# One buffer order for rotary and softmax, and the first key pair's rotation behind the second projection

## The reference, cut to what matters

```python
q = proj(Wq, bq); k = proj(Wk, bk); v = proj(Wv, bv)
q = _apply_rotary(q, cos, sin)      # per head, pairs of features
k = _apply_rotary(k, cos, sin)
attn = softmax(q @ k.T * scale)     # per head, 2048 x 2048
out = attn @ v
x = layernorm(x + out @ Wo.T + bo)
x = layernorm(x + moe(x))
```

## Time and profile before

| what | value |
|---|---|
| executions | 3115.75 and 3014.53 us, median 3065.14 |
| profiled execution | 3015.46 us; span of its slowest core (2) 3013.9 us |
| spans of the cores | 3002.6 to 3013.9 us, clock 0.950 to 0.953 |
| busy, core 2 | TensorE 2559.5 us (85%), VectorE 771.3 (26%), ScalarE 591.8 (20%), GpSimd 172.7 (6%) |
| chain that ended last | TensorE 74%, DMA 9%, VectorE 8%, issue 5%, ScalarE 4% |

### The profile page before, as it was taken

The page is one execution under the profiler, slowest core; times in us unless marked ns, Lnnn a source line. Parts: engine busy times, 40 slices in busy tenths (PEclk is TensorE's granted clock), DMA queues, the critical chain, the costliest instruction groups (busy, mean ns, idle before and its releaser), DMA issues.

```text
span 3013.9 us, 31163 instructions; the slowest of 8 cores (3002.6 to 3013.9 us)
## 1 busy us (share of the span) xinstructions
PE 2559.5 (85%) x12262; PEld 1189.2 (39%) x12262; DVE 771.3 (26%) x1140; ACT 591.8 (20%) x761; POOL 172.7 (6%) x323
## 2 busy tenths in 40 slices
PE   4778787888888888898499998999999899998993
PEld 3334343534353535343144443434444344443441
DVE  0222222222222222222722213131221312212226
ACT  0342424242424242432000000000000000000031
POOL 1000000000000000000001001010000101001000
PEclk9899999999999999998699999999999999999996
DMA  8310101010101010034034344444444444343423
GB/s 149 49 29 15 28 15 29 15 28 15 28 15 28 15 28 8 8 56 77 14 57 76 63 78 63 72 72 67 75 65 76 65 70 74 61 80 60 74 42 122
DMA packets 50720, 155.26 MB, mean 52 GB/s; under 512 B 6162, under 2 KB 6290, under 8 KB 49298
## 3 DMA queue, kind: packets, MB, share of 16 engines
q0 software_dynamic: 47264, 142.69, 29.0%
q1 hardware_dynamic: 3314, 10.59, 1.0%
HBM read 287.54 MB, written 8.39 MB: 98 GB/s over the span
## 4 chain that ended last, share of the span: by engine, by line
PE 74%; DMA 9%; DVE 8%; issue 5%; ACT 4%; DVEq 0%; ACTq 0%; POOL 0%; POOLq 0%
PE pb L792 15%; PE pb L809 14%; PE pb L866 9%; DMA wslab<-w_t 6%; PE pb L318 6%; PE pb L401 6%; PE pb L395 6%; PE pb L450 4%; PE pb L472 4%; PE pb L478 4%; PE pb L555 4%; DMA R_bf<-x_t 2%; ACT scr_bf L361 2%; ACT scr_bf L461 1%; DVE vbuf L639 1%
## 5 line engine op out<-in xcount | busy, mean ns | idle before, releaser
L866 PE MATMUL pb<-aog,wslab 128*128 128x512 bf16 x2048 | 458.5, 380 | 59.6 <-DMA wslab<-w_t 59.4
L792 PE MATMUL pb<-xy,wslab 128*128 128x512 bf16 x2048 | 466.2, 387 | 0.0
L809 PE MATMUL pb<-xy,wslab 128*128 128x512 bf16 x2048 | 452.5, 379 | 0.0
L803 ACT ACTIVATE scr_bf<-pb 128x512 bf16<-128x512 f32 x128 | 69.5, 594 | 1324.6 <-PE pb L792 1324.5
L866 PEld LDWEIGHTS pb<-aog,wslab 128*128 128x128 bf16 x2048 | 195.3, 98 | 319.2 <-issue 98.0
L461 ACT ACTIVATE scr_bf<-pb,mq_sb 128x1024 bf16<-128x1024 f32 x256 | 283.5, 1114 | 166.2 <-PE pb L478 114.4
L792 PEld LDWEIGHTS pb<-xy,wslab 128*128 128x128 bf16 x2048 | 203.0, 100 | 252.5 <-issue 20.7
L395 PE MATMUL pb<-R_bf,wslab 128*128 128x512 bf16 x768 | 293.4, 382 | 5.4 <-ACT vbuf L306 5.4
L809 PEld LDWEIGHTS pb<-xy,wslab 128*128 128x128 bf16 x2048 | 200.4, 98 | 241.6
L401 PE MATMUL pb<-R_bf,wslab 128*128 128x512 bf16 x768 | 293.1, 382 | 0.0
L879 DVE TENSOR_TENSOR R_f<-pb,R_f 128x512 f32<-128x512 f32 x256 | 177.1, 692 | 343.2 <-PE pb L866 329.9
(11 more groups left out here) (111 smaller groups left out, 1473.9 us busy)
## 6 DMA issues: line engine op xcount, KB each, us to landing
wslab<-w_t POOLq DMA_DIRECT2D x128, 512.0 KB, 5.6
wslab<-w_t POOLq DMA_DIRECT2D x128, 256.0 KB, 3.8
wslab<-wv_t POOLq DMA_DIRECT2D x8, 1024.0 KB, 9.3
R_bf<-x_t POOLq DMA_DIRECT2D x16, 512.0 KB, 7.2
wslab<-wq_t POOLq DMA_DIRECT2D x8, 1024.0 KB, 9.8
wslab<-wk_t POOLq DMA_DIRECT2D x8, 1024.0 KB, 9.7
wslab<-wo_t POOLq DMA_DIRECT2D x16, 512.0 KB, 5.3
y<-R_f SPq DMA_DIRECT2D x16, 512.0 KB, 2.6
```

Of the source, the lines that this page charges most:

```text
L792: last = t.matmul(pa[nc2].ap(), wslab.ap()[:, W1OFF[s1] + dc * 128: W1OFF[s1] + dc * 128 + 128], xy.ap()[:, dc * TL + nc2 * 512: dc * TL + ...
L809: last = t.matmul(pa[4 + nc2].ap(), wslab.ap()[:, W3OFF[s1] + dc * 128: W3OFF[s1] + dc * 128 + 128], xy.ap()[:, dc * TL + nc2 * 512: dc * ...
L866: last = t.matmul(pa[wb + nc2].ap(), wslab.ap()[:, W2OFF[s2] + fc * 128: W2OFF[s2] + fc * 128 + 128], aog.ap()[:, fc * TL + nc2 * 512: fc ...
```

## The change

- `emit_tail_pair` and `emit_evac_pair` use sb2 and sb3 for the evacuated pair and sb0 and sb1 for its squares, for all pairs.
- The tail of key pair 0 is issued behind the 32 matmuls of pair 2 and ahead of that pair's evacuation, no longer inside the matmuls.
- In `st_merged` the exponential of chunk kc writes the half kc % 2 (before: the other one), and is issued right behind scores(kc). TensorE's order becomes scores(0), scores(1), sums(0), then scores(kc), sums(kc-1), and at the end sums(15).

The number and the shapes of all instructions stay the same. The diff, cut to its core:

```diff
--- before.py
+++ after.py
@@ emit_tail_pair
-                    qso = 1024 if (a // 2) % 2 == 0 else 0
-                    qk = ["sb2", "sb3"] if qso else ["sb0", "sb1"]
...
-                            scr_bf.ap()[:, qso + q2 * 512: qso + q2 * 512 + 512],
+                            scr_bf.ap()[:, 1024 + q2 * 512: 1024 + q2 * 512 + 512],
...
-                            r=[qk[q2], "pswap"], w=[f"pa{2 + q2}"])
+                            r=[f"sb{2 + q2}", "pswap"], w=[f"pa{2 + q2}"])
...
-                        scr_f.ap()[:, 1024:2048], scr_bf.ap()[:, qso:qso + 1024],
+                        scr_f.ap()[:, 1024:2048], scr_bf.ap()[:, 1024:2048],
...
@@ emit_evac_pair
-                    A(lambda s, pbt=pbt, qso=qso: s.activation(
-                        scr_bf.ap()[:, qso:qso + 1024], pbt.ap(), AF.Identity,
+                    A(lambda s, pbt=pbt: s.activation(
+                        scr_bf.ap()[:, 1024:2048], pbt.ap(), AF.Identity,
...
-                        r=pbkeys + [bckey], w=qk)
+                        r=pbkeys + [bckey], w=["sb2", "sb3"])
+                    V(lambda v: v.tensor_tensor(
+                        scr_bf.ap()[:, 0:1024], scr_bf.ap()[:, 1024:2048],
+                        scr_bf.ap()[:, 1024:2048], ALU.mult),
+                        r=["sb2", "sb3"], w=["sb0", "sb1"])
...
@@ loop over pairs, behind T(pmm, ...)
-                        if dc == 2 and pr >= 1:
-                            emit_tail_pair(a - 2)
+                    if pr >= 1:
+                        emit_tail_pair(a - 2)
                     emit_evac_pair(a, pb_[pb[0] // 2],
                                    [f"pa{pb[0]}", f"pa{pb[1]}"])
@@ st_merged, emit_exp
-                    so = (1 - j) * 1024
...
-                        w=[f"sb{2 * (1 - j)}", f"sb{2 * (1 - j) + 1}"])
+                        w=[f"sb{2 * j}", f"sb{2 * j + 1}"])
...
@@ st_merged, order
                 emit_mms(0)
                 emit_mms(1)
                 if pre is not None:
                     pre()
                 emit_exp(0)
+                emit_exp(1)
+                sums_pvs(0)
                 for kc in range(2, NDC):
                     emit_mms(kc)
-                    emit_exp(kc - 1)
-                    if kc >= 2:
-                        sums_pvs(kc - 2)
-                emit_exp(NDC - 1)
-                sums_pvs(NDC - 2)
+                    emit_exp(kc)
+                    sums_pvs(kc - 1)
                 sums_pvs(NDC - 1)
```

More of the change, by code:

```diff
@@ L344, in emit_tail_pair @@
                         r=["pa2", "pa3", "sk"], w=["sf0", "sf1"])
-                    V(lambda v, a=a, qso=qso, cos=cos: v.tensor_tensor(
-                        scr_f.ap()[:, 1024:2048], scr_bf.ap()[:, qso:qso + 1024],
+                    V(lambda v, a=a, cos=cos: v.tensor_tensor(
+                        scr_f.ap()[:, 1024:2048], scr_bf.ap()[:, 1024:2048],
                         cos.ap()[:, a * 512: a * 512 + 1024], ALU.mult),
-                        r=qk + ["ck"], w=["sf2", "sf3"])
+                        r=["sb2", "sb3", "ck"], w=["sf2", "sf3"])
                     V(lambda v, a=a: v.tensor_tensor(
@@ L356, in emit_evac_pair @@
                 def emit_evac_pair(a, pbt, pbkeys):
[L357 to L360, removed]
-                    A(lambda s, pbt=pbt, qso=qso: s.activation(
-                        scr_bf.ap()[:, qso:qso + 1024], pbt.ap(), AF.Identity,
-                        bias=bcol.ap()[:, hh:hh + 1]),
-                        r=pbkeys + [bckey], w=qk)
[L365 to L368, removed]
+                    A(lambda s, pbt=pbt: s.activation(
+                        scr_bf.ap()[:, 1024:2048], pbt.ap(), AF.Identity,
+                        bias=bcol.ap()[:, hh:hh + 1]),
+                        r=pbkeys + [bckey], w=["sb2", "sb3"])
[3 more added lines that the diff above has]
+                        r=["sb2", "sb3"], w=["sb0", "sb1"])
                     for q2 in range(2):
-                        T(lambda t, q2=q2, sqo=sqo: t.matmul(
+                        T(lambda t, q2=q2: t.matmul(
                             pa[4 + q2].ap(), ones_sq.ap(),
-                            scr_bf.ap()[:, sqo + q2 * 512: sqo + q2 * 512 + 512],
+                            scr_bf.ap()[:, q2 * 512: q2 * 512 + 512],
                             start=True, stop=True),
-                            r=[sk_[q2], "ones"], w=[f"pa{4 + q2}"])
+                            r=[f"sb{q2}", "ones"], w=[f"pa{4 + q2}"])
                     if nt == 2:
@@ L445, in st_merged, with sums_pvs @@
             def st_merged(pre=None):
+                def sums_pvs(kc):
+                    j = kc % 2
+                    for qb in range(2):
+                        T(lambda t, kc=kc, j=j, qb=qb: t.matmul(
+                            pa[6 + qb].ap(), ones_sq.ap(),
+                            scr_bf.ap()[:, j * 1024 + qb * 512:
+                                        j * 1024 + qb * 512 + 512],
+                            start=(kc == 0), stop=(kc == NDC - 1),
+                            skip_group_check=True),
+                            r=[f"sb{2 * j + qb}", "ones"], w=[f"pa{6 + qb}"])
+                        T(lambda t, kc=kc, j=j, qb=qb, hl=hl: t.matmul(
+                            pa[4 + qb].ap(),
+                            vbuf.ap()[:, kc * 256 + hl * 128:
+                                      kc * 256 + hl * 128 + 128],
+                            scr_bf.ap()[:, j * 1024 + qb * 512:
+                                        j * 1024 + qb * 512 + 512],
+                            start=(kc == 0), stop=(kc == NDC - 1),
+                            skip_group_check=True),
+                            r=[f"sb{2 * j + qb}", f"vb{kc}"], w=[f"pa{4 + qb}"])
                 def emit_mms(kc):
@@ L459, in emit_exp @@
                     j = kc % 2
-                    so = (1 - j) * 1024
-                    A(lambda s, j=j, so=so: s.activation(
-                        scr_bf.ap()[:, so:so + 1024],
+                    A(lambda s, j=j: s.activation(
+                        scr_bf.ap()[:, j * 1024:(j + 1) * 1024],
                         pb[j].ap(), AF.Exp, bias=mq_sb.ap()[:, 6:7],
```

2 lines of the change are left out of this document (1 added, 1 removed).

## The result

| | before | changed kernel |
|---|---|---|
| median of the timed executions | 3015.6 us | 3065.4 us |
| profiled execution, span of the slowest core | 3013.9 us | 3065.6 us |
| median span of die 0, die 1 | 3011.5, 3005.0 | 3058.1, 3061.1 |

The ratio is 1.0171 with a 95% interval of 1.0158 to 1.0184, so the change costs about 51 us. I had forecast 3060 and a range of 3036 to 3082. Both executions timed before the prediction had left 3065 as the median of before; with more of them it is 3015.6, the profiled execution's time, so the sum had been made against the right number.

A forecast was written before the change was run, and what follows sets the result against it. TensorE, the fullest engine, was taken as the bound, losing time to waits behind the second key projection; 16 x (2.5 + 0.3 + 0) = 45 us on 3015.5 gave 3060 us, range 3036 to 3082.

The forecast's parts named there:

- part 1: Tail moved behind the second key projection: evacuation waits for cosine, square behind the add; each head 2.50 us later.
- ones-matmuls' wait: Sign: TensorE's wait for the square behind the second key projection grows by 16 x about 2.5, to 145 us.
- The 0.3 us for ones-matmuls at the low clock: Behind the second key projection: ones-matmuls run slow after longer TensorE idle time, +0.3 us a head.
- part 4: TensorE's clock: falls earlier behind the second key projection; ones-matmuls +0.3 us a head, low stretch in the loop 0.
- bounds of -1.4 and +1.0: Loop's low-clock stretch, us a head: ending at the same time gains 1.4, wholly covered by matmuls loses 1.0.
- +0.42 in place of +0.3: Ones-matmuls behind the second key projection wholly at the low clock, by the skill's rule; us a head, sum 3062.
- 2.5 to 3 us later after its last projection matmul: Sign: a head's first exponential comes this much later, otherwise the prediction is wrong as a whole.
- within 2%: Whole kernel's time differs from before by at most 2%, about 60 us; chance 0.79.
- clearly slower by the clock: Rival: ones-matmuls all at low clock, loop's low stretch fully covered; 63 us, 3079; chance 0.17.
- half of it back: Rival: the loop's low-clock stretch ends at the same time, so the loss is 22 us, 3038; chance 0.12.
- a tighter loop: Rival: exponentials issued in the order of their scores tighten the chunk loop; 45 - 37 = 8 us, 3024; chance 0.06.
- a hidden tail: Rival: evacuation and square behind the second key projection don't wait for the moved work; 3015; chance 0.03.

The follow-up runs named there:

- `loop_only`: Kernel before with only the new order of exponential and sums in the loop over chunks; spans of 3007.7 to 3010.9 us.
- the two filled kernels: Kernel before and changed kernel, each with useless matmuls in all of TensorE's gaps in a head; profiled executions 2986.0 and 3030.6 us.
- `tail_only`: Kernel before with only the tail of key pair 0 moved behind the 32 matmuls of pair 2; ratio 1.0184.
- `halves_only`: Kernel before with only the buffer edit: every pair evacuated into sb2 and sb3 and squared into sb0 and sb1; ratio 0.9997.
- `after_dc2`: Changed kernel with the tail of key pair 0 put back behind dc 2, the other two edits kept; ratio 1.0007.

## Why the prediction was right or wrong

**What was right.** The place of the loss (behind the second key projection), its sign, and its largest term: 37.4 of the 50.1 us are the delay of the square, where 2.5 a head gives 37.5. The steps of part 1 came out to a few hundredths in the head shown: sine 0.99 us behind the last projection matmul (0.98 forecast), cosine 1.14 behind it, evacuation 3.44 behind the last projection matmul (3.44 forecast), ones-matmuls' wait 146.0 us (145). The add had the longer gap of 0.46 us in this head, so its square is 2.77 late (3.20 behind the last projection matmul, which itself comes 0.43 earlier); most heads have the short gap (in two places only of the 48 adds was there an idle time). The 0.3 us for ones-matmuls at the low clock came out at 0.25 a head. One half for all pairs cost nothing alone. The loop cost nothing where it starts at the low clock (`loop_only`), and 0.13 us a head between the two filled kernels.

**A cause named in the wrong order.** I led with the evacuation that waits for the shared half, and noted the queue of VectorE beside it, with both ready 0.02 us apart. `tail_only` shows that the queue alone gives the delay, all but 0.06 us a head. The number was the same; the reason would have misled someone who then gave the evacuation a buffer of its own.

**What was wrong: the size of the clock's term, and what I took for measurable.** The sum had 0.3 us a head for ones-matmuls at the low clock and 0 for the rest of the clock, 4.5 us in 15 heads. It is 10.4. The step that failed is the "I take 0" of part 4: it looked only at the long gap and at where the one low stretch of a head would begin and end. The two things it asked about came out near the sum: the ones-matmuls cost 3.7 us (4.5 forecast), and the low stretch in the loop cost 5.1 us less than before, 0.34 a head and well inside the bounds of -1.4 and +1.0. What it had no term for is the projections, where low stretches that before doesn't have cost 11.8 us, behind short gaps as the 2.15 us after the query that had been harmless. Filling only those gaps took them away. That a later arrival moves every gap, and that this brings the clock down there, is my reading; no run shows what decides it. Of the rule cited from the Trainium skill ("TensorE: Matmul & The Clock Gate", section "HAM oscillation — how this bites in real kernels") the result it gave, +0.42 in place of +0.3, fits the head shown but not the mean of 0.25; its case is a long wait between bursts, and the low stretches in the projections came behind short ones.

The luck in the number: 3060 against 3065 is close because the two terms that were missing in the sum, +11.8 for the projections and +2.0 for the loop, met one of -5.1; in 15 heads the sum had 42.0 and the ruler gave 50.1. And one sign that I set was worded wrongly: "2.5 to 3 us later after its last projection matmul" left out that this matmul comes 0.43 us earlier, and it left out the low clock of the ones-matmuls. My own steps give 3.2; the mean of the heads is 3.2 (8.83 to 12.03), the head shown 3.61.

I called 2% about what a measurement can tell from no change. The interval is 0.13% wide to either side, and `halves_only` and `after_dc2` agree with before to 0.1%. The loss of 1.7% is far outside it. I gave 0.79 to "within 2%", which is where the ratio lies, but the sentence that the likeliest verdict is no change was wrong: it is a small, plain loss. The rivals: clearly slower by the clock (3079) went in the right direction with half of its size (10.4 us of the 21.3 that its 1.42 a head make in 15 heads), and in the projections, where it had nothing; half of it back, a tighter loop, and a hidden tail fell.

## What to carry to other kernels

Ask of every instruction that is moved which later one it now stands ahead of in its engine's queue; a moved product costs its place even when its data wait for nothing, and its cost is what the cover behind it no longer hides (the square is later by 0, 1.2 and 2.5 us a head with 13, 3 and 0 chunks of cover). Look in a latency chain for the instruction that waits in a queue behind work it doesn't need: here moving one 0.15 us instruction and a broadcast ahead of two products gave 35 us of the whole time. Measure on a ruler inside the stage, and where a clock can fall, compare kernels with the gaps filled before putting a difference down to delay.

## What the runs showed of the hardware that I had not expected

- The same idle time of about 2 us, with the same work around it, brings TensorE's clock down to 1.2 GHz in one kernel and leaves it at 2.4 in another, as the gap at 154 and at 160 us shows; what decides it is open. In the kernel before it fell at one place a head; in the changed kernel a projection that was fast ran its first 3.4 us at the low level. Here the clock's cost couldn't be read off the gap that was changed: 11.8 us arose in the projections.
- Useless matmuls in the gaps of the kernel before are worth their place: with 688 more of them in the stretch of the ruler (5570 against 4882), it takes 35.0 us less.
- Filling only some of the gaps gave a third of that, 12 us of the whole time, since the clock then fell in the others.
